# Causal mask partly written into the score stacks and partly moved to GpSimd, in a fused attention and expert layer

## The reference

```
x  = layernorm(xn) ;  Q, K, V = low-rank projections of x, 16 heads of 8
scores = einsum('bhse,bhte->bhst', Q, K) / sqrt(8)
scores = where(tril(ones(S, S)), scores, -1e9)        # causal
attn   = softmax(scores) ;  ctx = einsum('bhst,bhtd->bhsd', attn, V)
h  = xn + (ctx @ out_U @ out_V + out_b) ;  attention branch = h + mlp(layernorm(h))
out = x + attention branch + experts(xn)
```

## Time and profile before

| | |
|---|---|
| median of 3 runs | 983.79 us (980.91 to 986.04) |
| profiled execution | 975.54 us, span 973.8 us |
| busy in the span | PE 96%, DVE 71%, ACT 55%, POOL 52% |
| attention stage | 16 chunks from about 84 to 558 us |
| mean granted TensorE clock | 0.981 |

### The profile page before, as it was taken

How to read it: one execution, slowest core, us unless ns; L and a number is a source line. 1 busy time by engine, 2 the same in 40 slices (tenths; PEclk the granted TensorE clock), 3 DMA queues, 4 the chain that set the end, 5 groups by cost and what they waited for, 6 DMA issues and landing times. The chain is left out here.

```text
span 973.8 us, 25188 instructions
## 1 busy us (share of the span) xinstructions
PE 931.2 (96%) x7602; PEld 733.4 (75%) x7602; DVE 696.0 (71%) x3195; ACT 532.0 (55%) x1248; POOL 507.0 (52%) x677
## 2 busy tenths in 40 slices
PE   5689999999999999999999999999999999999997
PEld 5356665666666666666666589999999998989896
DVE  5868989878878778877878645555555554568887
ACT  2673555556655556655565645555555554554442
POOL 9342443577777777667777425544545444431010
PEclk8799999999999999999999999999999999999999
DMA  9486463554465554544442042222212222258874
GB/s 249 123 258 213 170 213 117 142 149 138 137 177 143 144 154 135 143 125 134 120 141 72 23 127 65 66 67 65 62 57 67 66 67 58 67 168 217 244 208 130
DMA packets 139765, 127.12 MB, mean 131 GB/s; under 512 B 17338, under 2 KB 121908, under 8 KB 139636
## 3 DMA queue, kind: packets, MB, share of 16 engines
q1 hardware_dynamic: 116336, 68.94, 26.4%
q0 software_dynamic: 20592, 56.43, 18.5%
q10 hardware_dynamic: 2708, 0.15, 0.2%
HBM read 57.15 MB, written 42.60 MB: 102 GB/s over the span
## 5 line engine op out<-in xcount | busy, mean ns | idle before, releaser
L1468 DVE CUSTOM_DVE_ANT_0 att_masked_st<-att_m_ps,att_mask_st 128x128 bf16<-128x128 f32 (+1 forms) x1024 | 308.6, 353 | 77.7 <-PE att_m_ps L1053 35.7
L862 ACT ACTIVATE att_probs<-att_t_ps 128x512 f32<-128x512 f32 x384 | 229.6, 599 | 182.6 <-PE att_t_ps L1075 146.4
L1710 POOL DMA_INDIRECT y_scratch<-moe_y,moe_row_now x136 | 131.6, 968 | 156.3 <-DVE moe_y L1964 114.8
L670 POOL DMA_INDIRECT slot_x<-xs,att_slot_now x128 | 128.1, 1001 | 66.2 <-PE att_t_ps L1075 32.0
L1958 DVE TENSOR_TENSOR moe_hidden<-moe_gate,moe_up_ps 128x352 f32<-128x352 f32 x136 | 70.9, 521 | 111.5 <-ACT moe_gate L1885 111.1
L1787 PE MATMUL moe_y_ps<-w_down,moe_hidden_t 128*128 (+1 forms) x816 | 114.5, 276 | 2.7 <-DVE moe_y L1964 2.2
L1885 ACT ACTIVATE moe_gate<-moe_gate_ps 128x352 f32<-128x352 f32 x136 | 63.1, 464 | 97.7 <-PE moe_up_ps L1770 97.7
L1787 PEld LDWEIGHTS moe_y_ps<-w_down,moe_hidden_t 128*128 128x128 f32 (+1 forms) x816 | 102.2, 192 | 4.4 <-issue 4.1
L677 POOL TENSOR_SCALAR_AFFINE_SELECT att_probs<-att_probs 128x512 f32<-128x512 f32 x120 | 77.6, 655 | 38.5 <-PE att_t_ps L1073 22.8
L1468 DVE DVE_READ_ACCUMULATOR2_ANT att_row_max<- 128x1 f32 x1024 | 84.4, 82 | 0.1
L1096 PE MATMUL att_pv_ps<-att_probs,att_v_ones 128*32 128x256 f32 x1024 | 81.8, 391 | 0.0
(11 more groups left out here) (269 smaller groups left out, 2105.8 us busy)
## 6 DMA issues: line engine op xcount, KB each, us to landing
att_k_stack<-att_qk_parts POOLq DMA_DIRECT2D x96, 128.0 KB
slot_x<-xs POOLq DMA_DIRECT2D x17, 516.0 KB, 3.6
xs<-slot_x SPq DMA_DIRECT2D x34, 258.0 KB, 2.9
xs<-xn_scratch SPq DMA_DIRECT2D x32, 256.0 KB
mlp_rows<-y_scratch POOLq DMA_DIRECT2D x16, 512.0 KB, 5.5
even_stack<-att_qk_parts SPq DMA_DIRECT2D x192, 32.0 KB
att_odd_stack<-att_qk_parts SPq DMA_DIRECT2D x192, 32.0 KB
first_words<-in_L_attn_hidden_states SPq DMA_DIRECT2D x8, 512.0 KB, 8.0
```

The lines of the kernel that those rows point to most:

```text
L670: pool.indirect_dma_start(env["slot_x"][:], bass.IndirectOffsetOnAxis(ap=slot_now[c.parity][:, col:col + 1], axis=0), xs[c.parity][:, t, k ...
L862: act.activation(probs[:, m % PT, :], t_ps[m % 2][:], ACT.Exp).then_inc(exp_done, 1)
L1468: last = dve.tensor_tensor_reduce(out=masked_st[m % 2][:, part], in0=m_ps[m % 2][:, part], in1=mask_st[:, SEQ - width:], scale=1.0, scalar ...
L1710: pool.indirect_dma_start(env["y_dram"][:], bass.IndirectOffsetOnAxis(ap=row_now[q.parity][:, t:t + 1], axis=0), y[c.parity][:], None).the ...
```

## The change

Three things change.

1. Rows 97 to 127 of both stacks, unused before, get constants at setup. Row 96+c (c from 1 to 31) of each Q stack is 1 at query 95+c of the first 128 queries of each sequence and 0 elsewhere; the same row of each K stack is -1e30 for the keys behind 95+c and 0 elsewhere. The score product now runs over 128 rows instead of 97, and it masks queries 96 to 126 by itself. The mask matmul of units 0 to 7 so covers 96 of 128 queries per lane: 192 columns instead of 256.
2. GpSimd writes those rows: two memsets of 32x2048, two selects of 32x4096 elements on the Q stacks and two of 32x1024 on the K stacks, ahead of the DMA of the row of ones. SP's first stack transfers now wait for the Q selects too (`cleared` and `other_cleared` at 2).
3. In chunks 3 to 10, `selected` also holds for units 6 and 7 of each sequence: 4 units per chunk, 32 in all, lose their mask matmul, and GpSimd gets 32 selects of 128x256 (two lanes of 128 queries), as the first work of pairs 3 and 9. `probs_times_v` of these units (n = 3 and 9, in slots 9 and 21) waits for GpSimd instead of ScalarE.

```diff
+        FIRST_SELECTED = [2 * GROUPS] * LATE + [2 * GROUPS - 2] * W_STEPS + [2 * GROUPS] * (chunks - 1 - LATE - W_STEPS) + [UNITS]
         def selected(c, u):
-            return u >= 2 * GROUPS and c.index < last_chunk
+            return FIRST_SELECTED[c.index] <= u
+        def selects_until(c, b, u):
+            earlier_ones = sum(2 * (UNITS - first) for first in FIRST_SELECTED[:c.index])
+            return earlier_ones + b * (UNITS - FIRST_SELECTED[c.index]) + u + 1 - FIRST_SELECTED[c.index]
...
-                    sp.wait_ge(cleared, 1)
-                    sp.wait_ge(other_cleared, 1)
+                    sp.wait_ge(cleared, 2)
+                    sp.wait_ge(other_cleared, 2)
...
                     pool.memset(rev_e[:, :, e], float(EXPERTS - e)).then_inc(first_ready, 1)
+                pool.wait_ge(first_ready, N_FIRST)
+                pool.wait_ge(const_ready, 5)
+                pool.wait_ge(v_cleared, 6)
+                pool.wait_ge(rows_ready, 1)
+                for b in range(2):
+                    pool.memset(k_stack[b][ROWS:P].bitcast(F32), 0.0).then_inc(k_rows_ready, 1)
+                pool.wait_ge(cleared, 1)
+                pool.wait_ge(other_cleared, 1)
+                for b in range(2):
+                    by_block = q_stack[b][ROWS:P].rearrange("p g i (q s) -> p (g i) q s", s=SEQ)[:, :, :, 0:P]
+                    pool.affine_select(out=by_block, in_=by_block, compare_op=ALU.not_equal, fill=1.0, base=ROWS - 1,
+                                       pattern=[[0, GROUPS * LANES], [0, 2], [-1, P]], channel_multiplier=1).then_inc((cleared, other_cleared)[b], 1)
+                pool.wait_ge(k_rows_ready, 2)
+                for b in range(2):
+                    by_block = k_stack[b][ROWS:P].rearrange("p g (q s) -> p g q s", s=SEQ)[:, :, :, 0:P]
+                    pool.affine_select(out=by_block, in_=by_block, compare_op=ALU.is_ge, fill=MASKED, base=ROWS - 1,
+                                       pattern=[[0, GROUPS], [0, 2], [-1, P]], channel_multiplier=1).then_inc(k_rows_ready, 1)
+                pool.wait_ge(k_rows_ready, 4)
+                pool.wait_ge(cleared, 2)
+                pool.wait_ge(other_cleared, 2)
...
-                    unit = probs[:, m % PT, :].rearrange("p (i s) -> p i s", i=LANES)
+                    lanes = LANES if m % UNITS >= 2 * GROUPS else 2
+                    unit = probs[:, m % PT, :].rearrange("p (i s) -> p i s", i=lanes)[:, :, 0:P]
...
-                    rows = slice(0, ROWS + 1)
+                    rows = slice(0, P)
...
-                        last = pe.matmul(by_lane[:, :, 0:P], ident_b[:], mask_ts[:, lanes, :], start=False, stop=True, skip_group_check=True)
+                        masked = slice(0, P if u >= 2 * GROUPS else ROWS)
+                        last = pe.matmul(by_lane[:, :, masked], ident_b[:], mask_ts[:, lanes, masked], start=False, stop=True, skip_group_check=True)
...
-                        pe.wait_ge(causal_done, GROUPS * (2 * c.index + b) + 2 * (u - GROUPS + 1))
+                        pe.wait_ge(causal_done, selects_until(c, b, 2 * u + 1))
```

More of the change, by code:

```diff
@@ L333, in first_and_attention @@
         const_ready, cleared, ones_ready = s.sem("const_ready"), s.sem("cleared"), s.sem("ones_ready")
+        k_rows_ready = s.sem("k_rows_ready")
         v_cleared, other_cleared = s.sem("v_cleared"), s.sem("other_cleared")
@@ L675, in keep_causal @@
                     pool.wait_ge(exp_done, 2 * UNITS * c.index + m + 1)
-                    unit = probs[:, m % PT, :].rearrange("p (i s) -> p i s", i=LANES)
+                    lanes = LANES if m % UNITS >= 2 * GROUPS else 2
+                    unit = probs[:, m % PT, :].rearrange("p (i s) -> p i s", i=lanes)[:, :, 0:P]
                     pool.affine_select(out=unit, in_=unit, compare_op=ALU.is_ge, fill=0.0, base=0,
-                                       pattern=[[0, LANES], [1, P]], channel_multiplier=-1).then_inc(causal_done, 1)
+                                       pattern=[[0, lanes], [1, P]], channel_multiplier=-1).then_inc(causal_done, 1)
                 def after_scores(p, slot):
```

## The result

The changed kernel takes 988.54 us in the median of 11 runs (984.53 to 994.78), the kernel before 980.91 in as many runs on the same chip (977.68 to 987.50): ratio 1.009, 95% interval 1.0065 to 1.0114. It is slower by 0.9%: 7.6 us between the two medians, 8.8 by the ratio, where +8.4 was forecast. The three runs that gave 983.79 are the first of these eleven, and the other eight brought the median down; the forecast's 992.2 is +0.85% on 983.79.

A forecast was written before the change was run, and what follows sets the result against it. TensorE's stream bounds the attention (VectorE sharing early), VectorE's chain alone the setup from 24 to 33 us. +12.9 - 1.8 - 2.7 = +8.4 us on the 983.79 median gives 992.2, forecast range 987 to 998, 984 to 999 with rivals.

The forecast's parts named there:

- Setup, +12.9: Setup: GpSimd's six added instructions, busy until about 39.3, hold VectorE's chain from 26.38 to 39.3; +12.9 us, bounds 0 and 14.5.
- the two variants: Setup: VectorE held throughout, 12.9 us late; or, second, passing one chain step between two GpSimd instructions, 12.3 to 13.
- Everything in the setup waits for it: Setup: everything behind VectorE's chain, the stores' queue included, waits for it, so no part of the delay is absorbed.
- The removed masks, -1.8: Attention, chunks 3 to 10: 32 mask matmuls go, 4.2 us, less 1.4 waiting for VectorE and 1.0 for GpSimd; -1.8 us.
- The narrower masks, -2.7: Attention: 224 masks lose 64 columns, 27 ns each won in odd slots; -2.7 us, bounds 0 and 6.0.
- in even slots ... 0.01 at most, taken as nothing: Attention, even slots: weights set a floor to the start behind a mask, so narrower masks win 0.01 us at most.
- The cover holds: Rival, setup: VectorE isn't held or itself holds GpSimd, whose selects stretch; -4.5 us, 979.3; chance 0.13.
- Half absorbed: Rival, setup: other paths or a later x set its end, loss 8 instead of 12.9; +3.5 net, 987.3; chance 0.1.
- GpSimd becomes the bound: Rival, chunks 3 to 10: pairs 5 and 11 read 0.5 late, removal loses 4 us; +14.2, 998; chance 0.07.
- the masks stay on TensorE: Rival, attention: the masks don't leave TensorE; held excluded by the order of instructions, no chance given.

The follow-up runs named there:

- the setup part alone: Kernel before plus the six GpSimd setup instructions and SP's longer waits, nothing reading the rows: 993.16 against 981.26 us, ratio 1.0109.
- in small pieces: Changed kernel with GpSimd's setup memsets and selects cut into pieces of 512 columns, against the kernel before: 983.23 against 980.85 us, ratio 1.0028.
- with memsets: Kernel before plus the six GpSimd setup instructions, the four selects replaced by same-size memsets, nothing reading the rows: 983.59 against 974.17 us, ratio 1.0085.
- ScalarE's rows: Changed kernel with ScalarE writing the constant rows and masks covering 97 queries, against the kernel before: ratio 0.9945; without the selects of units 6 and 7, 0.9967.

## Why the prediction was right

The forecast of 992.2 us and the 988.54 measured lie 0.4% apart, and the ratio, +0.9%, is the forecast's +0.85%. The main mechanism held; that the sum came out so close is in part luck, as the terms show.

- **Setup, +12.9.** The place, the engine and the mechanism held. The six instructions ran from 26.05 to 39.63, where 39.3 was forecast, with 3.88 and 3.87 for the Q selects (3.8 forecast); 32 partitions do take as long as 128. The first transpose came 11.9 late and slot 0 13.0. Of the two variants the second is what the trace shows: VectorE passes a step per GpSimd instruction. The steps passed were mis-sized: when GpSimd was done the chain stood at L159, 1.5 us of free chain behind L1283, where 0.6 at most had been granted. L159 started at 39.80, so the delay was 12.9 + 0.5 - 1.5 = 11.9 and not 12.3 to 13. The other 1.1 came behind the first transpose, where the same matmuls took 52.07 instead of 51.01 at a lower granted clock. With the setup part alone this second piece is 0.3 and slot 0 is 12.2 late: that 13.0 meets 12.9 is luck. What the prediction did not have is that the delay isn't GpSimd's occupied time: in small pieces GpSimd was busy longer and the kernel lost less. Nor is the whole setup tied to the first transpose: with memsets it moved 6.7 and slot 0 10.2, at a lower granted clock. "Everything in the setup waits for it" was right in direction only.
- **The removed masks, -1.8.** Slots 6 and 7 are 0.13 and 0.12 shorter, slot 8 0.08 longer while TensorE waits for VectorE (0.1 forecast). Pair 5 of chunk 9 waits for GpSimd: 0.47 in the fence above, slot 13 there 0.5 longer (0.5 forecast). The sum by starts is about 1 us, half of the forecast; whole runs give 2 to 5. The term is mis-sized in one way or the other, and why isn't settled.
- **The narrower masks, -2.7.** The 28 ns for 64 columns hold (27 forecast). A step that failed is "in even slots ... 0.01 at most, taken as nothing": the 121 ns behind a mask ahead of a full-width matmul became 93, so 256 columns had set that start and not the weights. It is a small step: even slots gave 0.43 us in chunks 3 to 10. With ScalarE's rows, whose setup costs nothing, the part brought 3.2 us by the ratio (2.1 to 4.3) and 3.1 by the starts of the whole attention.
- **Rivals.** "The cover holds" is refuted by L154's 3.91 us and by the run with the setup part alone. "Half absorbed" needed a later x; x came 1.6 later in this execution (L1308 at 26.30, its like at 24.67), and it absorbed nothing that shows: with the setup part alone x came 0.2 earlier (26.10), and L154 and the first transpose stand where they stand here. In the kernel before, the step that x allowed at 24.67 was held until 26.05 anyway. "GpSimd becomes the bound" didn't come: chunks 3 to 10 became shorter. With ScalarE's rows, where nothing else disturbs them, only chunks 5 and 9 are longer with the selects than without (29.57 against 29.34 and 29.33). In the kernel after, weight loads of L1132 waited 6.8 us in all for GpSimd, but the products themselves 1.3. That the masks stay on TensorE is refuted by the group's count, 224 instead of 256.
- **The parts.** Alone, the setup costs +1.09% (0.86 to 1.32) and both attention parts bring -0.55% (0.38 to 0.72): +0.54% together, give or take 0.29, where the whole gave +0.9% (0.65 to 1.14). The ranges overlap.

## What to carry to other kernels

Work that seems free because GpSimd idles is not free when VectorE walks a chain of short steps beside it: count the steps that are held and multiply by the length of one GpSimd instruction, up to GpSimd's whole time, and don't go by the share of time that is idle. If it must be there, cut it into pieces (here +0.9% became +0.28%), or give it to ScalarE where that idles (-0.55%). Before work is put on a DMA queue, look at what is queued behind it: here the engines were free and the kernel lost 6%.

## What the runs showed of the hardware

- Where GpSimd's instructions hold it, VectorE gets in for one step between two of them: L154 took 3.91 us beside a select of 3.88, 1.79 beside a memset of 1.8, 0.51 beside memsets of half a microsecond, 0.23 free.
- A GpSimd memset held a TENSOR_SCALAR (3.50 us) and not a TENSOR_TENSOR (0.29); a select held both (3.91 and 1.08).
- A ScalarE copy of 32x4096 elements takes 3.60 us and leaves VectorE's chain where it was (first transpose 32.79).
- TensorE's granted clock over the same matmuls, from the first transpose to slot 0, isn't told by the wait ahead of them: 0.83 in the kernel after and 0.91 with the setup part alone, both after a first transpose at 44.72; 0.79 with memsets, 0.77 in pieces; 0.88 in the kernel before.
- The issue of two broadcast transfers of 31 partitions by 8 runs of 512 bytes took SP 42.13 us, behind one of 31 by 32 such runs whose own issue took 0.87.
